# Cross-attention with image tokens on one core: the two parts of Z' summed by the matrix engine, and the image branch's steps moved to later slots

## The chip, the cores and the metric

The kernel runs on one core of one Trainium2 chip. The metric is the device time of one execution in microseconds (us). The engines are named as in the profile: PE is TensorE (PEld its weight loads), DVE is VectorE, ACT is ScalarE, POOL is GpSimd, SP is SyncE, which here issues the DMAs.

## The reference

Two attention layers follow each other. Each takes x (16 samples, 256 positions, 320 channels) and a context (16 samples, 256 rows, 512 channels), has 20 heads of 16 channels, and adds to a text attention a small attention over the context's last rows. The change is in the second layer only, in which 252 rows are text and the last 4 are image rows:

```python
q = heads(hidden_states @ W_q); k_t = heads(text_ehs @ W_k); v_t = heads(text_ehs @ W_v)
probs_t = softmax(q . k_t * scale)                     # per head, 256 x 252
text_out = probs_t @ v_t
k_ip, v_ip = heads(ip_ehs @ W_k_ip), heads(ip_ehs @ W_v_ip)
qsem = l2norm(probs_t @ text_ehs)                      # per head, 256 x 512, row by row
sem = qsem @ l2norm(ip_ehs).T
fused = q . k_ip * scale + 0.5 * sem
out = (text_out + (softmax(fused) * spatial_mask) @ v_ip) @ W_out + b_out + residual
```

The norm of `probs_t @ text_ehs` is needed for every head and position. The kernel does not form that product. It forms the Gram matrix G of the text rows once for each sample, and takes the squared norm as the sum over text rows of P times (G P), where P are the exponentials of the transposed scores.

## The kernel before, in words

`layer1` (line 655 on) runs one queue of instructions for each engine. All of them are written by the same loop over slots t, from T0 to T1, where slot t stands for head s = t of the running count of 16 x 20 = 320 (sample, head) pairs. An engine's order is the order in which its loop body writes things, slot after slot; engines are tied only by semaphore waits. Nothing is planned at run time. `AT` (line 659) gives the slot of each step that is done once for a sample; `due(t, off)` gives the sample that is due. The numbers of `AT` are read modulo 20 below: "slot 12" is the slot of a sample's 20 in which a step falls in the steady state.

In slot t, PE does in this order:

- NAT, the scores of head t+11 (line 736), from which DVE takes the row maxima MX (line 1063)
- every fourth slot (t = 2, 6, 10, 14, 18 modulo 20) the transposition of four heads' maxima into `rows` (line 747). `rows` is the right half of the PSUM bank PV. ACT (line 925) and DVE (line 1082, NH) read it; line 1082 counts semaphore `nm` up
- TR, the transposed scores of head t (line 757); ACT takes the exponential P (line 933) and a rounded copy PH (line 937)
- GP = G P of head t-2, six matmuls through the helper `product` (lines 768 to 772; in the trace they have the helper's line 60). It waits until DVE has read GP of the head before: there is one GP bank
- the group product PV for four heads (lines 773 to 791): 8 matmuls of VB with P into four column groups (line 787), then 4 matmuls of E21 with ZS (line 790), which put the squared norm into column 21 of each head's output. It stands in slots t = 3, 7, 11, 15, 19 modulo 20
- then the steps done once for a sample, on two PSUM banks MISC, taken in turn by a `Ring`: k (line 792), on (line 801), ptt, ipm, hst, om, q, gr, v, scm (lines 809 to 888), in this order within a slot. `take` makes a step wait until the bank's use before last has been read

DVE does in slot t: MX of head t+11, ZP = GP x PM of head t-2 (line 1071), PM = 2P - PH of head t-1 (line 1077), NH where it is due, and then the steps of `AT`. POOL adds the two halves of ZP (the two chunks of 128 text rows) into ZS (line 1221) and does the square roots (`pow`, line 1242), which DVE's `sem` steps (lines 1092 to 1125) wait for, and other subtractions and additions.

The group product's waits are, in order: the exponentials of its four heads, the read of PV by ACT (`pvs`), the count `nm`, and ZS:

```python
e.wait_ge(q["nm"], min(g + 4, B * NGRP))
e.wait_ge(q["zs"], HG * g + HG)
```

The group due at t = 4g + 7 waits for count g + 4 of `nm`. NH of group g + 3 is due at t = 4(g + 3) - 6 = 4g + 6.

Of the kernel before, what the change touches and what calls it, by code (L numbers as in the profile page):

```python
# [8 lines left out]
ALU = mybir.AluOpType  # L9
# [3 lines left out]
B, S, C, CD, H, D = 16, 256, 320, 512, 20, 16  # L13
T = 256
HG = 4
NGRP = H // HG
SLOT = 32
# [4 lines left out]
KC = CD // 128  # L22
# [17 lines left out]
def due_group(t, off):  # L40
    g, r = divmod(t - off, HG)
    return g if r == 0 and 0 <= g < B * NGRP else None
# [33 lines left out]
def stage(flat, n0, k):  # L76
    return flat[:, n0:n0 + k * C].rearrange("p (k n) -> p k n", n=C)
# [577 lines left out]
def layer1(nc, ctx, a, parts_h, vall, x1, x1_t, out):  # L655
    NT, NI, NV = T - 4, 4, D + 6
    N2 = NT - 128
    TRK = KM + 2
    AT = dict(q=(-3, 1, 5), k=(-2, 2, 6), spill=(-1, 3, 7), x_in=-22, xts=-12, c_in=-18, cts=-6, gr=(4, 8), v=(10, 12), kbd=12, scm=14,
              vip_in=20, vip=26, cmb=46, root=(46, 47, 48, 49), sem=(50, 51, 52), fu=53, tx=(54, 55, 56), ptt=56, ipm=59, hst=62, om=(69, 73), out=75,  # L660
              xb_in=59, xb=63)
    ONCE = -12
    NS, NZ, NIP = 4, 6, B * NI

    def sb(name, shape, dt=F32):
        return ctx.enter_context(nc.sbuf_tensor(name + "_1", shape, dt))
# [4 lines left out]
    def bank(name):  # L671
# [9 lines left out]
    MX, NH = sb("MX", [128, 2, 2, 8]), sb("NH", [4, 2, 2, S], F32R)  # L681
    P, PVS = sb("P", [128, NP, 2 * S]), sb("PVS", [128, S])
    PH, PM = sb("PH", [128, NS, 2 * S], F32R), sb("PM", [128, 2, 2 * S])
    ZP, ZS = sb("ZP", [128, 2, 2 * S]), sb("ZS", [128, NZ, S])
    GH, GL = sb("GH", [128, 2, 3, 128], F32R), sb("GL", [128, 2, 3, 128], F32R)
    E21, ONES, HALF = sb("E21", [128, SLOT]), sb("ONES", [128, 128]), sb("HALF", [128, NIP])
    ON = sb("ON", [128, 2, 2, H * NV])
# [10 lines left out]
    PV, GP = bank("PV"), bank("GP")  # L698
    ring = Ring([bank(f"MISC{k}") for k in range(2)])

    q = semaphores(nc, ctx, "s1_", "w_q w_k w_v w_rest w_sel sel x_in c_in xn_in spilled0 spilled1 spilled2 stack0 stack1 stack2 stack3 "
                   "stack4 mrow0 mrow1 store fill clear clear_q w_hi w_lo xt_hi xt_lo ct_hi ct_lo qk qk_f qk_hi qk_lo gr vc gh gl w_ip once once_s once_q rn "
                   "vall_out vip_in kbd scm sc vip vm v nat mx mxt nh nm tr exp ph pm gp zp zs pv pvs ont on cmb nrm fu fexp tx "
                   "ptt pt ipm hs hst ht_hi ht_lo om y xb")
    flat = P[:, :, :].rearrange("p r n -> p (r n)")
    q_raw, k_raw, v_raw = stage(flat, 0, 3), stage(flat, 3 * C, KC), stage(flat, (3 + KC) * C, KC)
    o_raw = stage(PM[:, :, :].rearrange("p r n -> p (r n)"), 0, 3)
    ki_raw = stage(ON[:, :, :, :].rearrange("p b a n -> p (b a n)"), 0, KC)
    vi_raw = stage(ZS[:, :, :].rearrange("p r n -> p (r n)"), 0, KC)
    once = XB[:, :, :].rearrange("p a n -> p (a n)")  # L710
    CIP, SQ = (once[:, n * KC * NIP:(n + 1) * KC * NIP].rearrange("p (k n) -> p k n", n=NIP) for n in range(2))
    VALL = HS[0:NIP, 0, :]
# [9 lines left out]
    def _(e):  # L722
        for t in range(T0, T1):
            s = t + LEAD
            if 0 <= s < B * H:
                b, h = divmod(s, H)
# [8 lines left out]
                for i in range(2):  # L735
                    ins = e.matmul(NAT[s % 2][:, i * T:(i + 1) * T], QS[0:KQ, h, i * 128:(i + 1) * 128],  # L736
                                   KS[0:KQ, h, :], start=True, stop=True)
                ins.then_inc(q["nat"], 1)
            g = due_group(t, HG - LEAD + 1)
            if g is not None:  # L740
# [5 lines left out]
                for i in range(2):  # L746
                    ins = e.transpose(rows[:, i * 128:(i + 1) * 128], MX[:, g % 2, i, 0:4], IDENT[:, :])  # L747
                ins.then_inc(q["mxt"], 1)
            s = t
            if 0 <= s < B * H:  # L750
                b, h = divmod(s, H)
# [4 lines left out]
                for i in range(2):  # L756
                    ins = e.matmul(TR[s % 2][:, i * S:(i + 1) * S], KS[0:TRK, h, i * 128:(i + 1) * 128],  # L757
                                   QS[0:TRK, h, :], start=True, stop=True)
                ins.then_inc(q["tr"], 1)
            s = t - 2  # L760
            if 0 <= s < B * H:
                b, h = divmod(s, H)
                p, k = b % 2, s % NS
# [3 lines left out]
                if s:  # L767
# [2 lines left out]
                product(e, GP[:, 0:S], [(GH[:, p, 0, :], p0), (GL[:, p, 0, :], p0)])  # L770
                product(e, GP[:, S:2 * S], [(GH[:, p, 1, :], p0), (GL[:, p, 1, :], p0), (GH[0:N2, p, 2, :], p1),
                                            (GL[0:N2, p, 2, :], p1)]).then_inc(q["gp"], 1)
            g = due_group(t, HG + 3)
            if g is not None:
                b, hg = divmod(g, NGRP)
                heads = [(j, HG * hg + j, (HG * g + j) % NP) for j in range(HG)]
                if hg == 0:
                    e.wait_ge(q["v"], 2 * (b + 1))
                    e.wait_ge(q["vc"], 2 * (b + 1))
                e.wait_ge(q["exp"], HG * g + HG)  # L780
                if g:
                    e.wait_ge(q["pvs"], g)
                e.wait_ge(q["nm"], min(g + 4, B * NGRP))
                e.wait_ge(q["zs"], HG * g + HG)
                for i in range(2):
                    for j, h, r in heads:
                        e.matmul(PV[SLOT * j:SLOT * (j + 1), 0:S], VB[:, b % 2, i, h, :], P[:, r, i * S:(i + 1) * S],  # L787
                                 start=i == 0, stop=False)
                for j, h, r in heads:
                    ins = e.matmul(PV[SLOT * j:SLOT * (j + 1), 0:S], E21[:, :], ZS[:, (HG * g + j) % NZ, :], start=False, stop=True)  # L790
                ins.then_inc(q["pv"], 1)
            for m, off in enumerate(AT["k"]):
                b = due(t, off)
# [7 lines left out]
            g = due_group(t, HG + 5)  # L801
            if g is not None:
# [3 lines left out]
                for i in range(2):  # L806
                    ins = e.transpose(k[:, i * 128:(i + 1) * 128], PVS[:, i * 128:(i + 1) * 128], IDENT[:, :])  # L807
                ins.then_inc(q["ont"], 1)
            b = due(t, AT["ptt"])
            if b is not None:  # L810
# [3 lines left out]
                for i in range(2):  # L814
                    ins = e.transpose(k[0:80, i * 128:(i + 1) * 128], FU[:, 1, i, :], IDENT[:, :])
                ins.then_inc(q["ptt"], 1)
            b = due(t, AT["ipm"])
# [8 lines left out]
            b = due(t, AT["hst"])  # L826
            if b is not None:
                for i in range(2):
# [4 lines left out]
                    for c, c0 in enumerate(CC):  # L833
                        ins = e.transpose(k[0:CK, c * 128:(c + 1) * 128], HS[:, i, c0:c0 + CK], IDENT[:, :])
                    ins.then_inc(q["hst"], 1)
            for i, off in enumerate(AT["om"]):
                b = due(t, off)
# [8 lines left out]
            for m, off in enumerate(AT["q"]):  # L846
                b = due(t, off)
# [58 lines left out]
    def _(e):  # L906
# [12 lines left out]
        for t in range(T0, T1):  # L919
# [7 lines left out]
            if 0 <= s < B * H:  # L927
# [7 lines left out]
                    e.wait_ge(q["gp"], s - NS + 1)  # L935
                e.wait_ge(q["exp"], s + 1)
                e.copy(PH[:, s % NS, :], P[:, s % NP, :]).then_inc(q["ph"], 1)  # L937
            g = due_group(t, HG + 3)
            if g is not None:
                if g:  # L940
                    e.wait_ge(q["ont"], g)
# [88 lines left out]
    def _(e):  # L1030
# [24 lines left out]
        for t in range(T0, T1):  # L1055
# [8 lines left out]
                                ALU.max).then_inc(q["mx"], 1)  # L1064
            s = t - 2
            if 0 <= s < B * H:
                if s >= 2:
                    e.wait_ge(q["zs"], s - 1)
                e.wait_ge(q["pm"], s + 1)
                e.wait_ge(q["gp"], s + 1)  # L1070
                e.tensor_tensor(ZP[:, s % 2, :], GP[:, :], PM[:, s % 2, :], ALU.mult).then_inc(q["zp"], 1)  # L1071
            s = t - 1
            if 0 <= s < B * H:
                if s >= 2:
# [131 lines left out]
    def _(e):  # L1206
# [4 lines left out]
            e.wait_ge(q["xt_hi"], c + 1)  # L1211
            e.tensor_tensor(XTS[1][0:CK, c, :], XT[0:CK, c, :], XTS[0][0:CK, c, :].bitcast(F32), ALU.subtract).then_inc(q["xt_lo"], 1)
        for t in range(T0, T1):
            s = t - 2
            if 0 <= s < B * H:
                if s == 0:
                    e.wait_ge(q["once"], 2)
                if s >= NZ:
                    e.wait_ge(q["pv"], (s - NZ) // HG + 1)
                e.wait_ge(q["zp"], s + 1)  # L1220
                e.tensor_tensor(ZS[:, s % NZ, :], ZP[:, s % 2, 0:S], ZP[:, s % 2, S:2 * S], ALU.add).then_inc(q["zs"], 1)  # L1221
            for m, off in enumerate(AT["k"]):
                b = due(t, off)
                if b is not None:
# [44 lines left out]
    def _(e):  # L1269
# [44 lines left out]
        for t in range(T0, T1):  # L1314
# [26 lines left out]
            if b is not None:  # L1341
                if b == 0:
                    e.wait_ge(q["vall_out"], 16)
                    e.wait_ge(q["sel"], 16)
                if b >= 2:
                    e.wait_ge(q["ipm"], 2 * (b - 1))
                e.dma_start(VIP[:, b % 2, :], vall[NI * b:NI * b + NI, :].unsqueeze(0).broadcast_to([H, NI, C])).then_inc(q["vip_in"], 16)
# [71 lines left out]
```

## Time and profile before

| | us |
|---|---|
| device time, 3 runs: median (lowest to highest) | 1891.41 (1887.83 to 1893.2) |
| device time of the profiled execution | 1883.8 |
| its span, first to last instruction | 1881.4 |
| PE busy | 1678.2 (89% of the span) |
| DVE busy | 1442.5 (77%) |
| ACT busy | 1038.3 (55%) |
| POOL busy | 869.7 (46%) |
| mean granted TensorE clock | 0.946 of 2.4 GHz |

The span is from the first to the last instruction of one profiled execution; what lies around it is 2.4 us. An engine's busy time is the time in which it had at least one instruction under way. The granted clock is 1 at 2.4 GHz and 0.5 at 1.2 GHz. A label such as GP or MISC is the tile that is written; what follows `<-` is what was read.

### The profile page before, as it was taken

Reading aid. Unit: us, or ns where it says so; the run is one execution under the profiler, and the core shown is the slowest. Engines: PE = TensorE matmul, PEld = TensorE weight load, DVE = VectorE, ACT = ScalarE, POOL = GpSimd, SP = SyncE. Lnnn points to the kernel's source line nnn. Section 1 sums busy time; section 2 is a strip of 40 time slices with the busy share of each in tenths; the row PEclk is TensorE's granted clock in tenths of the full one; section 3 lists DMA queues with packets and bytes.
Section 4 is the critical chain, followed back from the end, with each engine's and each line's share of the span. In section 5 each row is a group of like instructions: output and inputs, shape, how many; then the busy total and the mean of one; then the engine's idle time right before and its main releaser. Section 6 shows DMA issues by size and latency. Waiting matters only on the chain.

```text
span 1881.4 us, 42185 instructions
## 1 busy us (share of the span) xinstructions
PE 1678.2 (89%) x14344; PEld 1479.0 (79%) x14344; DVE 1442.5 (77%) x3732; ACT 1038.3 (55%) x2188; POOL 869.7 (46%) x714
## 2 busy tenths in 40 slices
PE   5999999999999997479899888988988898898985
PEld 4888888888888885468788787877878787887864
DVE  4677777777777776458878887887888788787884
ACT  3566666666666665236556555555555554554551
POOL 4232332333332222455666566556555645655553
PEclk9999999999999999689999999999998998998997
DMA  6334444444444332633223313322331322231210
GB/s 170 106 113 115 123 120 117 120 120 118 118 122 113 116 102 66 177 89 90 57 68 97 86 45 90 90 67 67 87 85 46 91 81 58 74 98 53 60 33 21
DMA packets 186492, 172.65 MB, mean 92 GB/s; under 512 B 25884, under 2 KB 186282, under 8 KB 186282
## 3 DMA queue, kind: packets, MB, share of 16 engines
q1 hardware_dynamic: 186282, 169.97, 32.5%
q8 instruction: 117, 1.92, 0.5%
q14 instruction: 93, 0.76, 0.1%
HBM read 110.19 MB, written 57.59 MB: 89 GB/s over the span
## 4 chain that ended last, share of the span: by engine, by line
PE 31%; DVE 11%; POOL 7%; issue 7%; ACT 3%; SPq 1%; DMA 0%; DVEq 0%; ACTq 0%; POOLq 0%
PE MISC L60 12%; PE GP L60 9%; POOL NRM L1242 3%; PE NAT L736 3%; DVE ZP L1071 3%; DVE PM L1077 2%; PE TR L757 2%; POOL ZS L1221 2%; PE PV L787 2%; DVE MX L1063 1%; PE PV L790 1%; PE MISC L807 1%; PE PV L747 1%; ACT P L933 1%; DVE HS L1150 1%
## 5 line engine op out<-in xcount | busy, mean ns | idle before, releaser
L1221 POOL TENSOR_TENSOR ZS<-ZP 128x256 f32<-128x256 f32 x320 | 312.0, 975 | 402.0 <-DVE ZP L1071 402.0
L314 ACT ACTIVATE P<-TA 128x512 f32<-128x512 f32 x320 | 201.9, 632 | 252.5 <-DVE TA L460 251.9
L60 PE MATMUL GP<-PH,GH 128*128 128x256 f32 (+1 forms) x960 | 262.2, 300 | 86.1 <-DVE ZP L1071 67.9
L1071 DVE TENSOR_TENSOR ZP<-GP,PM 128x512 f32<-128x512 f32 x320 | 219.7, 686 | 68.6 <-PE GP L60 55.1
L60 PEld LDWEIGHTS GP<-PH,GH 128*128 128x128 f32 (+1 forms) x960 | 190.9, 199 | 99.3 <-issue 60.6
L60 PE MATMUL GP<-PH,GL 128*128 128x256 f32 (+1 forms) x960 | 254.6, 292 | 0.0
L1077 DVE SCALAR_TENSOR_TENSOR PM<-P,PH 128x512 f32<-128x512 f32 x320 | 247.0, 772 | 0.0
L1063 DVE TENSOR_REDUCE MX<-NAT 128x2 f32<-128x504 f32 x320 | 215.8, 675 | 19.3 <-PE NAT L736 16.1
L445 DVE TENSOR_REDUCE MX<-NAT 128x2 f32<-128x154 f32 x320 | 101.9, 318 | 167.7 <-PE NAT L142 165.8
L933 ACT ACTIVATE P<-TR 128x512 f32<-128x512 f32 x320 | 190.0, 594 | 58.1 <-PE TR L757 54.2
L460 DVE TENSOR_TENSOR TA<-TR,ST 128x512 f32<-128x512 f32 x320 | 219.2, 686 | 3.0 <-PE TR L162 2.8
L937 ACT CAST PH<-P 128x512 fp32r<-128x512 f32 x320 | 198.4, 620 | 28.2 <-PE GP L60 0.4
L60 PEld LDWEIGHTS GP<-PH,GL 128*128 128x128 f32 (+1 forms) x960 | 193.3, 201 | 0.1
L449 DVE CUSTOM_DVE_ANT_0 TMP<-NAT,SN 128x179 f32<-128x179 f32 x640 | 192.0, 337 | 0.4 <-issue 0.2
L526 POOL TENSOR_TENSOR PARTS<-QKF,PARTS 112x512 fp32r<-112x512 f32 (+1 forms) x48 | 61.4, 1280 | 225.5 <-ACT PARTS L332 225.5
L736 PE MATMUL NAT<-KS,QS 65*128 65x256 f32 x640 | 148.4, 316 | 11.4 <-DVE MX L1063 11.4
L142 PE MATMUL NAT<-KS,QS 65*128 65x256 f32 x640 | 151.3, 319 | 5.4 <-DMA KS<-qk_parts 5.4
L757 PE MATMUL TR<-QS,KS 67*128 67x256 f32 x640 | 139.8, 301 | 0.0
L736 PEld LDWEIGHTS NAT<-KS,QS 65*128 65x128 f32 x640 | 106.1, 200 | 39.8 <-issue 26.1
L162 PE MATMUL TR<-QS,KS 69*128 69x256 f32 x640 | 135.4, 294 | 0.2
L142 PEld LDWEIGHTS NAT<-KS,QS 65*128 65x128 f32 x640 | 103.1, 191 | 39.4 <-issue 21.4
L1242 POOL TENSOR_TENSOR NRM<-NRM,HALF 128x10 f32<-128x10 f32 x64 | 132.0, 2064 | 2.5 <-DVE NRM L1090 2.5
(229 smaller groups left out, 4402.7 us busy)
## 6 DMA issues: line engine op xcount, KB each, us to landing
QS<-qk_parts SPq DMA_DIRECT2D x480, 64.0 KB, 2.7
qk_parts<-PARTS SPq DMA_DIRECT2D x96, 224.0 KB, 2.6
CT<-in_ctx_t SPq DMA_DIRECT2D x32, 512.0 KB, 4.2
KS<-qk_parts SPq DMA_DIRECT2D x240, 64.0 KB, 2.7
KS<-qk_parts SPq DMA_DIRECT2D x240, 63.0 KB, 2.9
qk_parts<-PARTS SPq DMA_DIRECT2D x48, 192.0 KB, 2.3
QS<-NH SPq DMA_DIRECT2D x480, 4.0 KB
qk_parts<-PARTS SPq DMA_DIRECT2D x32, 220.5 KB, 3.9
```

Of the source, the lines that this page charges most:

```text
L60: ins = e.matmul(out, lhs, rhs, start=(n == 0), stop=(n == len(pairs) - 1))
L142: ins = e.matmul(NAT[s % 2][:, i * T:(i + 1) * T], QS[0:KQ, h, i * 128:(i + 1) * 128], KS[0:KQ, h, :], start=True, stop=True)
L314: e.activation(P[:, s % NP, :], TA[:, s % 2, :], ACT.Exp, scale=SCALE).then_inc(q["exp"], 1)
L449: ins = e.tensor_tensor_reduce(TMP[:, k, i, :], v[:, i, NT:T], SN[:, b % 2, i, :], 1.0, -3.0e38, ALU.add, ALU.max, MX[:, g % 2, i, HG + j: ...
L460: e.tensor_tensor(TA[:, s % 2, :], TR[s % 2][:, :], ST[:, b % 2, :], ALU.add).then_inc(q["sum"], 1)
L736: ins = e.matmul(NAT[s % 2][:, i * T:(i + 1) * T], QS[0:KQ, h, i * 128:(i + 1) * 128], KS[0:KQ, h, :], start=True, stop=True)
L933: e.activation(P[:, s % NP, :], TR[s % 2][:, :], ACT.Exp, scale=SCALE).then_inc(q["exp"], 1)
L937: e.copy(PH[:, s % NS, :], P[:, s % NP, :]).then_inc(q["ph"], 1)
L1063: e.tensor_reduce(MX[:, g % 2, :, j], NAT[k][:, :].rearrange("p (a t) -> p a t", a=2)[:, :, 0:NT], AX.X, ALU.max).then_inc(q["mx"], 1)
L1071: e.tensor_tensor(ZP[:, s % 2, :], GP[:, :], PM[:, s % 2, :], ALU.mult).then_inc(q["zp"], 1)
L1077: e.scalar_tensor_tensor(PM[:, s % 2, :], P[:, s % NP, :], 2.0, PH[:, s % NS, :].bitcast(F32), ALU.mult, ALU.subtract).then_inc(q["pm"], 1)
L1221: e.tensor_tensor(ZS[:, s % NZ, :], ZP[:, s % 2, 0:S], ZP[:, s % 2, S:2 * S], ALU.add).then_inc(q["zs"], 1)
```

## The change

- The six ZS buffers and POOL's addition (line 1221) go. DVE's ZP has five buffers instead of two; DVE waits for `pv` instead of `zs` before it writes one again. PE's E21 product runs over both halves of ZP: 8 matmuls for a group instead of 4.
- The group product on PE and ACT's copy of its result are due at `HG + 2` instead of `HG + 3`: t = 4g + 6, one slot earlier. It waits for `zp` instead of `zs`. The wait for `nm` stays as it is.
- Of the steps of `AT`, sem goes from (50, 51, 52) to (52, 53, 54), fu 53 to 55, tx (54, 55, 56) to (56, 57, 58), ptt 56 to 59, ipm 59 to 61, hst 62 to 64, vip 26 to 32. root, cmb, om, out and the others stay.
- SP waits for `vip` of the sample before ahead of the load of VIP.

```diff
--- before.py
+++ after.py
@@ -657,10 +657,10 @@
     N2 = NT - 128
     TRK = KM + 2
     AT = dict(q=(-3, 1, 5), k=(-2, 2, 6), spill=(-1, 3, 7), x_in=-22, xts=-12, c_in=-18, cts=-6, gr=(4, 8), v=(10, 12), kbd=12, scm=14,
-              vip_in=20, vip=26, cmb=46, root=(46, 47, 48, 49), sem=(50, 51, 52), fu=53, tx=(54, 55, 56), ptt=56, ipm=59, hst=62, om=(69, 73), out=75,
+              vip_in=20, vip=32, cmb=46, root=(46, 47, 48, 49), sem=(52, 53, 54), fu=55, tx=(56, 57, 58), ptt=59, ipm=61, hst=64, om=(69, 73), out=75,
               xb_in=59, xb=63)
     ONCE = -12
-    NS, NZ, NIP = 4, 6, B * NI
+    NS, NZ, NIP = 4, 5, B * NI
 
     def sb(name, shape, dt=F32):
         return ctx.enter_context(nc.sbuf_tensor(name + "_1", shape, dt))
@@ -681,7 +681,7 @@
     MX, NH = sb("MX", [128, 2, 2, 8]), sb("NH", [4, 2, 2, S], F32R)
     P, PVS = sb("P", [128, NP, 2 * S]), sb("PVS", [128, S])
     PH, PM = sb("PH", [128, NS, 2 * S], F32R), sb("PM", [128, 2, 2 * S])
-    ZP, ZS = sb("ZP", [128, 2, 2 * S]), sb("ZS", [128, NZ, S])
+    ZP = sb("ZP", [128, NZ, 2 * S])
     GH, GL = sb("GH", [128, 2, 3, 128], F32R), sb("GL", [128, 2, 3, 128], F32R)
     E21, ONES, HALF = sb("E21", [128, SLOT]), sb("ONES", [128, 128]), sb("HALF", [128, NIP])
     ON = sb("ON", [128, 2, 2, H * NV])
@@ -700,13 +700,13 @@
 
     q = semaphores(nc, ctx, "s1_", "w_q w_k w_v w_rest w_sel sel x_in c_in xn_in spilled0 spilled1 spilled2 stack0 stack1 stack2 stack3 "
                    "stack4 mrow0 mrow1 store fill clear clear_q w_hi w_lo xt_hi xt_lo ct_hi ct_lo qk qk_f qk_hi qk_lo gr vc gh gl w_ip once once_s once_q rn "
-                   "vall_out vip_in kbd scm sc vip vm v nat mx mxt nh nm tr exp ph pm gp zp zs pv pvs ont on cmb nrm fu fexp tx "
+                   "vall_out vip_in kbd scm sc vip vm v nat mx mxt nh nm tr exp ph pm gp zp pv pvs ont on cmb nrm fu fexp tx "
                    "ptt pt ipm hs hst ht_hi ht_lo om y xb")
     flat = P[:, :, :].rearrange("p r n -> p (r n)")
     q_raw, k_raw, v_raw = stage(flat, 0, 3), stage(flat, 3 * C, KC), stage(flat, (3 + KC) * C, KC)
     o_raw = stage(PM[:, :, :].rearrange("p r n -> p (r n)"), 0, 3)
     ki_raw = stage(ON[:, :, :, :].rearrange("p b a n -> p (b a n)"), 0, KC)
-    vi_raw = stage(ZS[:, :, :].rearrange("p r n -> p (r n)"), 0, KC)
+    vi_raw = stage(ZP[:, :, :].rearrange("p r n -> p (r n)"), 0, KC)
     once = XB[:, :, :].rearrange("p a n -> p (a n)")
     CIP, SQ = (once[:, n * KC * NIP:(n + 1) * KC * NIP].rearrange("p (k n) -> p k n", n=NIP) for n in range(2))
     VALL = HS[0:NIP, 0, :]
@@ -770,7 +770,7 @@
                 product(e, GP[:, 0:S], [(GH[:, p, 0, :], p0), (GL[:, p, 0, :], p0)])
                 product(e, GP[:, S:2 * S], [(GH[:, p, 1, :], p0), (GL[:, p, 1, :], p0), (GH[0:N2, p, 2, :], p1),
                                             (GL[0:N2, p, 2, :], p1)]).then_inc(q["gp"], 1)
-            g = due_group(t, HG + 3)
+            g = due_group(t, HG + 2)
             if g is not None:
                 b, hg = divmod(g, NGRP)
                 heads = [(j, HG * hg + j, (HG * g + j) % NP) for j in range(HG)]
@@ -781,13 +781,15 @@
                 if g:
                     e.wait_ge(q["pvs"], g)
                 e.wait_ge(q["nm"], min(g + 4, B * NGRP))
-                e.wait_ge(q["zs"], HG * g + HG)
+                e.wait_ge(q["zp"], HG * g + HG)
                 for i in range(2):
                     for j, h, r in heads:
                         e.matmul(PV[SLOT * j:SLOT * (j + 1), 0:S], VB[:, b % 2, i, h, :], P[:, r, i * S:(i + 1) * S],
                                  start=i == 0, stop=False)
-                for j, h, r in heads:
-                    ins = e.matmul(PV[SLOT * j:SLOT * (j + 1), 0:S], E21[:, :], ZS[:, (HG * g + j) % NZ, :], start=False, stop=True)
+                for i in range(2):
+                    for j, h, r in heads:
+                        ins = e.matmul(PV[SLOT * j:SLOT * (j + 1), 0:S], E21[:, :], ZP[:, (HG * g + j) % NZ, i * S:(i + 1) * S],
+                                       start=False, stop=i == 1)
                 ins.then_inc(q["pv"], 1)
             for m, off in enumerate(AT["k"]):
                 b = due(t, off)
@@ -935,7 +937,7 @@
                     e.wait_ge(q["gp"], s - NS + 1)
                 e.wait_ge(q["exp"], s + 1)
                 e.copy(PH[:, s % NS, :], P[:, s % NP, :]).then_inc(q["ph"], 1)
-            g = due_group(t, HG + 3)
+            g = due_group(t, HG + 2)
             if g is not None:
                 if g:
                     e.wait_ge(q["ont"], g)
@@ -1064,11 +1066,13 @@
                                 ALU.max).then_inc(q["mx"], 1)
             s = t - 2
             if 0 <= s < B * H:
-                if s >= 2:
-                    e.wait_ge(q["zs"], s - 1)
+                if s >= NZ:
+                    e.wait_ge(q["pv"], (s - NZ) // HG + 1)
                 e.wait_ge(q["pm"], s + 1)
                 e.wait_ge(q["gp"], s + 1)
-                e.tensor_tensor(ZP[:, s % 2, :], GP[:, :], PM[:, s % 2, :], ALU.mult).then_inc(q["zp"], 1)
+                if s == 0:
+                    e.wait_ge(q["once"], 2)
+                e.tensor_tensor(ZP[:, s % NZ, :], GP[:, :], PM[:, s % 2, :], ALU.mult).then_inc(q["zp"], 1)
             s = t - 1
             if 0 <= s < B * H:
                 if s >= 2:
@@ -1211,14 +1215,6 @@
             e.wait_ge(q["xt_hi"], c + 1)
             e.tensor_tensor(XTS[1][0:CK, c, :], XT[0:CK, c, :], XTS[0][0:CK, c, :].bitcast(F32), ALU.subtract).then_inc(q["xt_lo"], 1)
         for t in range(T0, T1):
-            s = t - 2
-            if 0 <= s < B * H:
-                if s == 0:
-                    e.wait_ge(q["once"], 2)
-                if s >= NZ:
-                    e.wait_ge(q["pv"], (s - NZ) // HG + 1)
-                e.wait_ge(q["zp"], s + 1)
-                e.tensor_tensor(ZS[:, s % NZ, :], ZP[:, s % 2, 0:S], ZP[:, s % 2, S:2 * S], ALU.add).then_inc(q["zs"], 1)
             for m, off in enumerate(AT["k"]):
                 b = due(t, off)
                 if b is not None:
@@ -1342,6 +1338,8 @@
                 if b == 0:
                     e.wait_ge(q["vall_out"], 16)
                     e.wait_ge(q["sel"], 16)
+                if b:
+                    e.wait_ge(q["vip"], b)
                 if b >= 2:
                     e.wait_ge(q["ipm"], 2 * (b - 1))
                 e.dma_start(VIP[:, b % 2, :], vall[NI * b:NI * b + NI, :].unsqueeze(0).broadcast_to([H, NI, C])).then_inc(q["vip_in"], 16)
```

## Rows read from the trace of the kernel before

**Rows 1.** Waits of 900 to 1700 us: us in total, times, longest

```profile
PE MISC L834 <- ACT PARTS L955: 10.6, 12, 0.9
...
PE PV L787 <- POOL ZS L1221: 7.6, 13, 1.3
```

**Rows 2.** Instructions in time (start us, us): PE, slot 7 of two samples

```profile
1217.72 0.41 PE L736 MATMUL NAT<-KS,QS 65*128 65x256 f32 x2
...
1283.32 0.41 PE L736 MATMUL NAT<-KS,QS 65*128 65x256 f32 x2
```

**Rows 3.** In time, PE: the starts of slots 3 and 4

```profile
1272.36 0.48 PE L736 MATMUL NAT<-KS,QS 65*128 65x256 f32 x2
...
1275.15 0.51 PE L736 MATMUL NAT<-KS,QS 65*128 65x256 f32 x2
```

**Rows 4.** Chain of waits (start us, us, what), slot 3

```profile
1273.08 0.71 PE GP L60 x6
1273.79 1.00 PE PV L787 x16
1274.79 0.43 PE PV L790 x8
```

**Rows 5.** In time, PE and DVE: slot 6, from GP's end on

```profile
1281.93 0.28 PE L60 MATMUL MISC<-CTSH,WKH 128*96 128x252 f32 x1
...
1282.23 0.69 DVE L1071 TENSOR_TENSOR ZP<-GP,PM 128x512 f32<-128x512 f32 x1 [0.52 <-PE GP L60]
1282.84 0.68 DVE L1077 SCALAR_TENSOR_TENSOR PM<-P,PH 128x512 f32<-128x512 f32 x1
1283.43 0.41 DVE L1082 SCALAR_TENSOR_TENSOR NH<-PV,NH 4x256 fp32r<-4x256 f32 x1
```

**Rows 6.** In time, PE and DVE: ipm in slot 19; ZP, then the next GP

```profile
1262.26 1.34 PE L825 MATMUL MISC<-VIP,PT 80*128 80x320 f32 x4
...
1264.95 0.69 DVE L1071 TENSOR_TENSOR ZP<-GP,PM 128x512 f32<-128x512 f32 x1
...
1265.78 0.36 PE L60 MATMUL GP<-PH,GH 128*128 128x256 f32 x1 [0.49 <-DVE ZP L1071]
```

**Rows 7.** Groups of instructions of 900 to 1700 us: busy us, mean ns, idle before

```profile
L1157 DVE TENSOR_TENSOR HTL<-MISC,HTH 112x384 fp32r<-112x384 f32 x24 | 13.4, 558 | 16.7 <-ACT HTH L982 15.6
```

**Rows 8.** In time, DVE and PE: slot 12

```profile
1232.65 0.72 DVE L1096 TENSOR_TENSOR NRM<-NRM,RZ 128x40 f32<-128x40 f32 x1 [3.55 <-POOL NRM L1242]
...
1236.08 0.44 PE L60 MATMUL GP<-PH,GH 128*128 128x256 f32 x1 [3.06 <-DVE ZP L1071]
```

**Rows 9.** In time, POOL, DVE, PE: slots 14 to 17

```profile
1246.46 2.38 POOL L1255 TENSOR_TENSOR CTSL<-CT,CTSH 128x1024 fp32r<-128x1024 f32 x1
...
1246.92 2.09 DVE L1134 TENSOR_SCALAR FM<-FM,MASK 128x20 f32<-128x20 f32 x2
...
1250.57 0.36 PE L60 MATMUL GP<-PH,GH 128*128 128x256 f32 x1 [1.46 <-ACT PH L937]
...
1253.14 0.44 PE L60 MATMUL GP<-PH,GH 128*128 128x256 f32 x1 [0.33 <-DVE ZP L1071]
```

**Rows 10.** Chain of waits, behind the last head: line 1134 again

```profile
1865.67 0.39 DVE FM L1134 x2
```

**Rows 11.** Stretches: length, busy PE, PEld, DVE, ACT, POOL, PEclk, DMA share, GB/s

```profile
1232.77:1236.19 3.42, 0.36 (x4) 0.18 (x3) 3.32 (x7) 1.27 (x3) 2.02 (x4) 1.00 0.20 57
1236.19:1239.60 3.41, 3.41 (x15) 3.41 (x16) 3.31 (x7) 0.00 (x0) 1.46 (x2) 0.50 0.00 0
...
1249.84:1253.25 3.41, 1.92 (x13) 1.60 (x14) 3.41 (x6) 1.40 (x3) 1.16 (x2) 1.00 0.41 116
1253.25:1256.67 3.42, 3.42 (x17) 3.42 (x18) 3.40 (x5) 1.12 (x3) 1.40 (x2) 0.50 0.00 0
1270.32:1273.73 3.41, 2.52 (x23) 2.15 (x21) 2.02 (x5) 2.52 (x5) 2.31 (x2) 1.00 0.10 9
1273.73:1277.15 3.42, 3.42 (x41) 2.67 (x41) 2.85 (x5) 2.06 (x4) 2.11 (x2) 1.00 0.78 263
```

## The prediction

> **What bounds the kernel now.** I read three views: the table of waits, the instructions in order of time over one sample's 20 slots (two starts of slot 7 are 65.6 us apart [rows 2]), and stretches with the clock. The reader is to see that PE is nearly always at work and that its losses in a sample stand in a few places. In slot 12 DVE waits for POOL's square roots, and PE then waits 3.06 us for ZP [rows 8]. In slots 14 to 17 DVE is crowded: line 1134's two small instructions take 2.09 us while POOL's CTSL runs, and PE waits 1.46 and 0.33 us [rows 9]; alone the same two take 0.39 [rows 10]. Both places are followed by 3.4 us at granted clock 0.50 [rows 11]. Small losses: the product waits for ZS 7.6 us and hst for a bank 10.6 us in 800 us [rows 1], which is 12.2 samples, so 0.6 and 0.9 us a sample. So the order of PE's queue sets the time, and any new wait in it counts in full.
>
> **The step that decides: the count `nm`.** The group product moves to t = 4g + 6 but still waits for count g + 4 of `nm`. That count is given by NH of group g + 3, which DVE does at t = 4(g + 3) - 6 = 4g + 6. Before, a slot lay between the two; now they stand in the same one. The wait is not a spare: `rows` and the product share the bank PV. In that slot DVE does NH behind ZP and PM, and ZP needs this slot's GP. Slot 6 shows the chain: GP's last matmul has been issued and the next starts at 1281.93; ZP starts at 1282.23, PM at 1282.84, NH at 1283.43 and takes 0.41 [rows 5], so it ends at 1283.84. From a DVE end to PE's start behind it 0.14 pass (ZP ends at 1265.64, GP starts at 1265.78 [rows 6]). The product can start at 1283.98: PE stands still for 2.05 us. Behind it in PE's queue are the rest of the slot (k, v, scm) and the next slot's NAT, TR and GP, so nothing of PE's fills the gap; ACT's copy of PV, and ACT's later steps with it, wait too, but ACT is idle for 45% of the span. Five products a sample: 5 x 2.05 = 10.2 us. The bounds are 0, if something I don't see covers it, and 2.7 where GP itself runs at half clock and so ends 0.7 later (its 0.71 [rows 4] doubled).
>
> **The other costs, for one sample.**
> - E21 over both halves: today's four products take 0.43 us on PE [rows 4]; the same again in each group, 5 x 0.43 = 2.15.
> - Slots 3, 7, 11, 15, 19 lose the product. Slot 3 was 2.79 us long [rows 3], and without 1.43 of it [rows 4] 1.36 would be left. But there is one GP bank: GP 0.71 [rows 4], 0.30 to ZP [rows 5], ZP 0.69 and 0.14 to the next GP [rows 6] make 1.84 us a head at the least. So 0.48 in each of the five can't be had: 2.4. (Below nothing it can't be; 0 if DVE's work there is still delayed from before.)
> - hst comes into slot 4, ahead of gr, and there are two MISC banks: gr's take waits for hst's first bank, which DVE reads in HTL, in this same slot behind ZP and PM. From GP's end: 0.30 + 0.61 + 0.60 [rows 5], HTL 0.56 [rows 7], 0.14: 2.2 us, of which the transpositions cover some 0.8. Taken 1.4, bounds 0 and 2.2.
> - ipm comes into slot 1, between on and q. q's take waits for DVE's read of the first ipm bank, again behind ZP and PM: 1.5, an addition taken like HTL's 0.56, and 0.14, so 2.2 us, covered by on and the ipm products, which take 1.34 with their tail [rows 6]. Taken 1.1 with the wait of the second ipm for on's bank; bounds 0 and 2.2.
> - The later vip, fu and ptt are off PE's path. SP's new wait is for a multiplication that stands 8 slots ahead of the load, and nothing behind it in SP's queue is short of time: 0, at most the 0.8 us that one DMA's issue takes, which no one waits for.
>
> Sum of costs: 10.2 + 2.15 + 2.4 + 1.4 + 1.1 = 17.3.
>
> **The gains, for one sample.** The roots of slots 6 to 9 have until slot 12 instead of 10, and POOL has no ZS between them: the wait of 3.06 goes, and with it a stretch of 3.41 at half clock [rows 8, 11], worth half, 1.7: 4.8. What is late next there is v, which PE does at once. In slots 14 to 17: line 1134 moves to slot 16, away from CTSL, and no ZS runs beside DVE; 1.46 + 0.33 + 1.7 (half of the slow 3.42 [rows 11]) go, and I leave 0.8 for slot 16, where DVE's reduction, reciprocal and 1134 still come on top of the three large ones: 2.7. The waits for ZS and for hst's bank go: 0.6 + 0.9. POOL's 312 us in themselves give nothing. Sum 9.0.
>
> What a page says of POOL beside DVE: the Trainium skill, SBUF — State Buffer, "Who interferes with whom", has it that a DVE instruction with two SBUF inputs and a POOL instruction that reads SBUF shut each other out for the whole instruction. The trace agrees: 2.09 beside CTSL against 0.39 alone. By that rule sem's additions, now in slot 14 with CTSL, can be held up by its 2.4 us; that would fall under PE's product and scm, and the sum would be the same.
>
> **The clock.** The stretch with 3.06 us of waiting and the one between 1249.84 and 1253.25, in which PE had the wait of 0.33 and most of that of 1.46 and was busy for 1.92 us of 3.41 were each followed by half clock; the one with 0.9 of waiting (PE busy 2.52) was not [rows 11]. A wait of 2.05 is nearer to the first two. There are seven new places of over 1 us in a sample. I take four falls, and 1.5 us each (half of 3.41 is 1.7, less what PE would have waited anyway): 6.0. Bounds: none, and seven at 1.7, 11.9.
>
> **The sum.** A sample costs 17.3 - 9.0 = 8.3 us more at full clock, and 6.0 for the clock. The last four products need no further NH, so 76 of 80 groups wait, 15.2 samples: 15.2 x 14.3 = 217. On the profiled execution's own 1883.8 that is 2101. Behind the last head no load stands beside the chain, and one or two ZS of 1 us go: 2100. The median of the runs shown is 7.6 above the profiled one and the three differ by 5.4; I leave that in the range.
>
> **Rivals.**
> - *The clock holds.* Same waits, no falls: 1883.8 + 15.2 x 8.3 = 2010. For it: single waits of 0.9 left the clock whole, and the new ones are apart, with busy slots between them. Against: the waits of 1.46 and 0.33 were enough in slots 16 and 17. The Trainium skill, TensorE: Matmul & The Clock Gate, "HAM oscillation — how this bites in real kernels", warns of idle gaps longer than any of the new waits; by that rule the clock would hold, and it would be this rival. The trace of slots 16 and 17 speaks against the rule. Chance 0.2.
> - *The wait on `nm` is covered,* so the time falls. One mechanism: NH would have to be done by GP's end in its slot. Then 10.2 and the 6.0 go, and a sample changes by 7.1 - 9.0 = -1.9: 1883.8 - 29 = 1855. It decides itself in slots 2, 6, 10, 14, 18: below 0.4 us of wait in each (15.2 x 5 x 0.4 = 30) the kernel is faster. For it: POOL's wait of ZP is gone and DVE is freer. Against: NH stands behind ZP in DVE's order, and ZP can't start before GP ends. Chance 0.05.
> - *The clock stays low for longer:* each new wait falls into a slow stretch and keeps it going, seven falls or more: 1883.8 + 15.2 x (8.3 + 11.9) = 2191. For it: at half clock GP ends later and NH with it. Against: after a slow stretch of full work the clock came back at once. Chance 0.05.
> - *The edit does less than it says:* DVE's crowding in slots 14 to 17 stays (CTSL now beside sem), and a part of the five waits takes the place of waits on ZP that PE had anyway. Then the balance is near nothing to +60: 1885 to 1945. Chance 0.05, a third of it within 0.3% of before.
>
> **How the numbers follow.** The forecast has 0.65, with its own range of 2040 to 2150. The range of 8 in 10 is 2000 to 2155: it takes in the rival of the full clock and leaves out the covered wait, the weak edit and the far end. 0.3% is about what a measurement of this kernel can tell from no change. Faster 0.05, within it 0.02, slower 0.93.
>
> **What would show it.** In the trace of after: the first of line 787's products with 1.9 to 2.1 us of idle time before it, released by DVE NH L1082, about 76 times; the second half of the E21 products adding 0.43; DVE no longer waiting for NRM; L1134 at about 0.4 for two; PE waiting before gr in slot 4 for HTL and before q in slot 1 for HS; a mean clock well under 0.946. A sample's length in the steady state is to be 78 to 81 us. The prediction is wrong if the products start right behind GP, or if the clock stays at 1.00 around them.

## The result and the profile after

The changed kernel takes 2153.49 us (median of 4 runs, 2151.58 to 2171.32) against 1889.62 us before (4 runs, 1886.59 to 1893.2): a ratio of 1.1414, 95% interval 1.1381 to 1.1447. It is slower by 264 us where 209 were forecast (2100 against 1891.41). The median lies at the very end of the range of 2000 to 2155, and the ratio times the 1891.41 on which the forecast stood is 2159, just outside. The profiled execution took 2154.05 us against 1883.8.

From the page of the changed kernel, engines and busy tenths:

```profile
span 2151.9 us, 42844 instructions
PE 1792.0 (83%) x14984; PEld 1538.6 (71%) x14984; DVE 1393.4 (65%) x3732; ACT 1030.2 (48%) x2188; POOL 562.4 (26%) x394
PE   5999999999999847877787787877787877877875
PEclk9999999999999977999889988999888997998887
```

The first layer (the first 14 slices or so) is as it was. In the second, POOL has lost its 312 us of additions, PE works 114 us more and still is busy for a smaller share: 83% instead of 89%.

The groups of instructions over the whole execution (busy us, mean ns, idle time before and its releaser):

```profile
L787 PE MATMUL PV<-P,VB 128*32 128x256 f32 x1280 | 112.6, 479 | 157.5 <-DVE NH L1086 157.5
L791 PE MATMUL PV<-ZP,E 128*32 128x256 f32 x1280 | 120.0, 498 | 0.0
L60 PE MATMUL MISC<-CTSH 128*128 128x256 f32 (+1 forms) x128 | 43.8, 342 | 40.0 <-DVE HTL L1161 40.0
L1081 DVE SCALAR_TENSOR_TENSOR PM<-P,PH 128x512 f32<-128x512 f32 x320 | 264.2, 826 | 0.0
```

The first row is the predicted wait: 157.5 us of PE standing still ahead of the group product, released by NH. Slot 6 in order of time, PE and DVE:

```profile
1411.11 0.28 PE L60 MATMUL GP<-PH,GL 124*128 124x256 f32 x1
...
1411.53 0.69 DVE L1075 TENSOR_TENSOR ZP<-GP,PM 128x512 f32<-128x512 f32 x1 [0.59 <-PE GP L60]
1412.14 0.68 DVE L1081 SCALAR_TENSOR_TENSOR PM<-P,PH 128x512 f32<-128x512 f32 x1
1412.74 0.41 DVE L1086 SCALAR_TENSOR_TENSOR NH<-PV,NH 4x256 fp32r<-4x256 f32 x1
...
1413.39 1.07 PE L787 MATMUL PV<-P,VB 128*32 128x256 f32 x16 [2.00 <-DVE NH L1086]
1414.25 1.07 PE L791 MATMUL PV<-ZP,E 128*32 128x256 f32 x16
```

It is the chain of [rows 5], now with the product at its end. A product begins 0.65 us after NH has begun. The next view is of slots 2 to 4 of the changed kernel, POOL, DVE and PE, where the forecast was too low:

```profile
1479.54 1.27 POOL L1223 TENSOR_TENSOR PARTS<-QKF,PARTS 112x508 fp32r<-112x508 f32 x1 [15.80 <-ACT PARTS L957]
1480.77 1.55 POOL L1227 TENSOR_TENSOR XB<-XB,BIAS 128x640 f32<-128x640 f32 x1
...
1480.23 2.64 DVE L1081 SCALAR_TENSOR_TENSOR PM<-P,PH 128x512 f32<-128x512 f32 x1
...
1484.58 1.01 DVE L1161 TENSOR_TENSOR HTL<-MISC,HTH 112x384 fp32r<-112x384 f32 x2
...
1485.18 0.58 PE L60 MATMUL MISC<-CTSH 128*128 128x256 f32 x1 [3.11 <-DVE HTL L1161]
```

PM, 0.68 us elsewhere [rows 5], takes 2.64: it begins while POOL's PARTS runs and ends 0.55 us behind XB. HTL stands behind it and one more MX, ZP and PM in DVE's queue, and PE waits 3.11 us for it ahead of gr. Last the clock, stretches of the changed kernel (columns as in [rows 11]), with the product at 1442.49 in the first's end:

```profile
1439.40:1442.84 3.44, 1.44 (x18) 1.20 (x20) 3.39 (x8) 1.47 (x3) 0.00 (x0) 0.99 0.00 0
1442.84:1446.25 3.41, 3.41 (x35) 1.83 (x26) 0.33 (x1) 0.20 (x1) 0.00 (x0) 0.51 0.27 99
```

One wait for NH alone is followed by a stretch at half clock, in which the product takes 1.75 us instead of 1.07. Work at half clock loses half of its time, so (1 - mean clock) x span is about what the clock costs: 0.084 x 2151.9 = 181 us after, 0.054 x 1881.4 = 102 before, 79 more. PE's busy time agrees: it grew by 114 us, of which 35 are the second half of the E21 product, whose rows follow in the section on the prediction. The next three stretches are of slots 3 to 6 of one sample; the wait of 3.11 us ahead of gr ends at 1403.62, in the second:

```profile
1398.47:1401.88 3.41, 1.61 (x12) 1.39 (x12) 3.41 (x4) 2.56 (x5) 2.29 (x2) 0.98 0.46 129
1401.88:1405.29 3.41, 1.67 (x8) 1.67 (x9) 2.15 (x5) 0.00 (x0) 0.00 (x0) 0.50 0.44 124
1405.29:1408.71 3.42, 3.42 (x19) 3.42 (x18) 1.08 (x3) 1.75 (x5) 0.00 (x0) 0.52 0.00 0
```

Here one fall lasts for two stretches. Between 900 and 2098 us, 14.3 samples, 78 of 351 such stretches are at half clock, in 58 falls; in the kernel before, between 902 and 1837 us, 14.0 samples, it is 35 of 274, in 25 falls.

### The profile page after: what moved, and what is told of

The parts are those of the page before. It is cut to its first block, busy times and chain, and to the rows that moved or that the text cites. A ratio compares the mean times of both kernels' runs of the same rounds, so it can differ in the third digit from the quotient of the medians.

```text
span 2151.9 us, 42844 instructions
## 1 busy us (share of the span) xinstructions
PE 1792.0 (83%) x14984; PEld 1538.6 (71%) x14984; DVE 1393.4 (65%) x3732; ACT 1030.2 (48%) x2188; POOL 562.4 (26%) x394
## 4 chain that ended last, share of the span: by engine, by line
PE 39%; DVE 14%; ACT 5%; issue 5%; POOL 1%; SPq 1%; DMA 0%; DVEq 0%; ACTq 0%; POOLq 0%
PE MISC L60 14%; PE GP L60 8%; DVE PM L1081 6%; PE PV L787 5%; PE PV L791 5%; DVE ZP L1075 4%; PE NAT L736 3%; ACT PH L939 2%; PE TR L757 2%; ACT P L935 2%; DVE MX L1065 1%; PE MISC L888 1%; DVE NH L1086 1%; ACT NH L927 1%; PE PV L747 1%
## 5 line engine op out<-in xcount | busy, mean ns | idle before, releaser
L60 PE MATMUL GP<-PH,GH 128*128 128x256 f32 (+1 forms) x960 | 267.9, 306 | 62.9 <-DVE ZP L1075 61.4
L1081 DVE SCALAR_TENSOR_TENSOR PM<-P,PH 128x512 f32<-128x512 f32 x320 | 264.2, 826 | 0.0
L787 PE MATMUL PV<-P,VB 128*32 128x256 f32 x1280 | 112.6, 479 | 157.5 <-DVE NH L1086 157.5
L1223 POOL TENSOR_TENSOR PARTS<-QKF,PARTS 112x508 fp32r<-112x508 f32 (+1 forms) x48 | 61.0, 1271 | 693.7 <-ACT PARTS L957 693.7
L945 ACT COPY PVS<-PV 128x256 f32<-128x256 f32 x80 | 29.8, 372 | 329.9 <-PE PV L791 329.9
L787 PEld LDWEIGHTS PV<-P,VB 128*32 128x32 f32 x1280 | 46.0, 124 | 187.4 <-issue 180.2
L142 PE MATMUL NAT<-KS,QS 65*128 65x256 f32 x640 | 150.8, 318 | 4.8 <-DMA KS<-qk_parts 4.6
L736 PE MATMUL NAT<-KS,QS 65*128 65x256 f32 x640 | 140.8, 305 | 11.2 <-DVE MX L1065 11.2
L1238 POOL TENSOR_TENSOR NRM<-NRM,HALF 128x10 f32<-128x10 f32 x64 | 137.4, 2164 | 37.6 <-DVE NRM L1094 37.6
```

The source lines that it names most:

```text
L60: ins = e.matmul(out, lhs, rhs, start=(n == 0), stop=(n == len(pairs) - 1))
L1081: e.scalar_tensor_tensor(PM[:, s % 2, :], P[:, s % NP, :], 2.0, PH[:, s % NS, :].bitcast(F32), ALU.mult, ALU.subtract).then_inc(q["pm"], 1)
```

## The experiments

Each is timed against the kernel before on the same chip. From chip to chip the kernel before took 1887 to 1894 us, so a difference between medians of two experiments is good to some 7 us; where it matters, compare the ratios. "NH" is the step at line 1082 of the kernel before.

**e1: NH ahead of ZP and PM in DVE's order, in the changed kernel.**

```diff
@@ block.vector, behind the reduction to MX
+            g = due_group(t, HG - LEAD + 1)
+            if g is not None:
+                e.wait_ge(q["nh"], g + 1)
+                e.scalar_tensor_tensor(NH[0:4, g % 2, 1, :], rows, -1.0, NH[0:4, g % 2, 0, :].bitcast(F32), ALU.mult, ALU.subtract).then_inc(q["nm"], 1)
             s = t - 2
...
@@ block.vector, behind PM
-            g = due_group(t, HG - LEAD + 1)
-            if g is not None:
-                e.wait_ge(q["nh"], g + 1)
-                e.scalar_tensor_tensor(NH[0:4, g % 2, 1, :], rows, -1.0, NH[0:4, g % 2, 0, :].bitcast(F32), ALU.mult, ALU.subtract).then_inc(q["nm"], 1)
```

> The changed kernel with DVE's NH (and so the count nm) put ahead of ZP and PM in its slot; nothing else moves. Theory (the product's wait for nm in its own slot is the loss): the idle time ahead of the product, 157 us in all, falls to under 20 us, some of the clock falls go with it, and the time drops from 2153 to 1900-1990 us. Rival (the doubled E21 product and the bank waits of the moved steps are the loss, and nm only shows it): the time stays above 2110 us.

Measured: 1971.34 us (1962.42 to 1976.82), ratio 1.0427 (1.0392 to 1.0461). The product's group and slot 6:

```profile
L787 PE MATMUL PV<-P,VB 128*32 128x256 f32 x1280 | 87.2, 389 | 34.5 <-DVE NH L1070 26.3 <-ACT P L935 8.2
```

```profile
1410.74 0.41 DVE L1070 SCALAR_TENSOR_TENSOR NH<-PV,NH 4x256 fp32r<-4x256 f32 x1
...
1411.40 1.07 PE L787 MATMUL PV<-P,VB 128*32 128x256 f32 x16 [0.21 <-ACT P L935]
```

The order of two DVE steps alone is worth 182 us of the 264. PE's idle time there falls from 157.5 to 34.5 us, 123 less. Its busy time falls from 1792.0 to 1737.6 us, 54 less for the same work, since the mean clock is 0.940 instead of 0.916. Together that is the 177 us between the two profiled spans. The time is in the expected range, but more of the wait is left than the 20 us expected.

**e2: the kernel before with only the product and ACT's copy one slot earlier.**

```diff
-            g = due_group(t, HG + 3)
+            g = due_group(t, HG + 2)     # on PE and on ACT
```

> The kernel before with the group product and the copy of its result one slot earlier (t = 4g + 6), and nothing else: POOL's addition, the single E21 product and all slots of AT stay. Theory: each product waits about 2.05 us for nm, the slots it leaves are held to 1.84 us by the one GP bank, and the clock falls more often: 2060-2150 us from 1890. Rival (the single early slot is harmless without the other edits): 1880-1900 us.

Measured: 2171.2 us (2167.02 to 2174.11), ratio 1.15 (1.1471 to 1.1528). It is 21 us above the expected range. This one number of the slot makes all of the loss and more, with POOL's addition, the single E21 product and the old slots in place.

```profile
L787 PE MATMUL PV<-P,VB 128*32 128x256 f32 x1280 | 103.8, 446 | 186.1 <-POOL ZS L1221 182.1 <-DVE NH L1082 4.0
```

```profile
1404.72 1.03 POOL L1221 TENSOR_TENSOR ZS<-ZP 128x256 f32<-128x256 f32 x1 [2.40 <-DVE ZP L1071]
...
1405.09 0.41 DVE L1082 SCALAR_TENSOR_TENSOR NH<-PV,NH 4x256 fp32r<-4x256 f32 x1
...
1405.75 1.07 PE L787 MATMUL PV<-P,VB 128*32 128x256 f32 x16 [2.00 <-POOL ZS L1221]
```

The view names ZS, since that addition ended last (1405.75). But it is the addition for a head of the next group, which this product does not ask for, and the product begins 0.66 us after NH begins, as it does in the changed kernel, which has no ZS. So I read the releaser as NH here too; it is a reading of the times, no run takes ZS out of this kernel. A wait of several semaphores is put down to the last event near it, and this is how it misleads.

**e3: the new slots alone, in the kernel before.**

```diff
-              vip_in=20, vip=26, ... sem=(50, 51, 52), fu=53, tx=(54, 55, 56), ptt=56, ipm=59, hst=62, ...
+              vip_in=20, vip=32, ... sem=(52, 53, 54), fu=55, tx=(56, 57, 58), ptt=59, ipm=61, hst=64, ...
```

> The kernel before with the new slots of AT (sem, fu, tx, ptt, ipm, hst, vip and SP's wait) and nothing else. Theory: the waits for the square roots and in slots 14 to 17 go with their slow stretches (8.4 us a sample), new bank waits before gr and q come (about 3.9 us a sample): 1810-1860 us. Rival (the moves cost more than they bring): 1890-1930 us.

Measured: 1884.19 us (10 runs), ratio 0.9974 (0.9954 to 0.9995): next to nothing, a miss of 24 us and more. The waits of 1000 to 1700 us, and slots 2 to 4 of one sample, POOL first, then DVE and PE:

```profile
PE MISC L60 <- DVE HTL L1157: 30.6, 11, 2.9
PE GP L60 <- DVE ZP L1071: 29.2, 37, 2.0
```

```profile
1018.32 1.29 POOL L1227 TENSOR_TENSOR PARTS<-QKF,PARTS 112x508 fp32r<-112x508 f32 x1 [0.61 <-ACT PARTS L955]
1019.56 0.74 POOL L1221 TENSOR_TENSOR ZS<-ZP 128x256 f32<-128x256 f32 x1
1020.25 1.56 POOL L1231 TENSOR_TENSOR XB<-XB,BIAS 128x640 f32<-128x640 f32 x1
1019.02 3.33 DVE L1077 SCALAR_TENSOR_TENSOR PM<-P,PH 128x512 f32<-128x512 f32 x1
1024.67 0.39 PE L60 MATMUL MISC<-CTSH 128*128 128x256 f32 x1 [2.90 <-DVE HTL L1157]
```

DVE's wait for the roots, 3.55 us in a sample before [rows 8], is gone from the list, but the bank wait ahead of gr costs 2.8 us a sample, and the mean clock is 0.938, no better than 0.946. What the roots gave went into the wait that the moves made. PM of slot 3 is held up here too, for 3.33 us beside PARTS, ZS and XB, although POOL has its addition ZS as before.

**e4: the changed kernel with the old slots of AT** (the diff of e3 the other way round).

> The changed kernel with all slots of AT as before. Theory: the waits for the roots have been hidden by now, since POOL has no addition and the slots are longer, so the moves bring nothing here and the bank wait before gr (3.1 us a sample) goes: 2090-2140 us. Rival (the moves are still worth what they are worth in the kernel before): 2200 us or more.

Measured: 2093.01 us (2091.27 to 2097.66), ratio 1.1091 (1.1065 to 1.1116). In the changed kernel the moves cost 60 us. Without them the wait ahead of gr is gone: PE is idle for 39 us less (321.0 against 359.9) and busy for 23 us less, at a mean clock of 0.930. DVE does wait for the roots again, 2.2 us in a sample, but no wait of PE for ZP between 1000 and 1700 us is longer than 1.3 us, where the kernel before has 3.1.

**e5 and e11: POOL's addition to XB two slots later, and two slots earlier, in the changed kernel.**

```diff
-              xb_in=59, xb=63)
+              xb_in=59, xb=65)      # e5
+              xb_in=59, xb=61)      # e11
```

> The changed kernel with POOL's addition of the bias to XB two slots later (slot 5 instead of 3), nothing else. Theory (PM in slot 4 waits 2 us for POOL's PARTS and XB, which run one behind the other, and HTL and gr wait behind it): PM of slot 4 falls to about 1.1 us at most, the wait ahead of gr from 3.1 to about 1.5 us a sample, the time from 2153 to 2105-2135 us. Rival (HTL is late for its own reasons, ACT's HTH or the banks): the wait stays near 3.1 and the time within 10 us of 2153.

> The changed kernel with POOL's addition to XB ahead of PARTS of slot 2 in POOL's queue (slot 1 instead of 3), nothing else. In e5 it was put behind, and as nothing else stood in POOL's queue it ran right behind PARTS all the same. Theory (PM of slot 3 waits for PARTS and XB one behind the other): that PM falls from 2.64 to about 1.1 us, the wait ahead of gr from 3.1 to about 1.6 us, the time from 2153 to 2110-2140 us. Rival (PM's length is not what holds gr): the wait stays at 3.1 us and the time within 12 us of 2153.

Measured: e5 2165.39 us (2165.18 to 2168.0), ratio 1.1438 (1.141 to 1.1466); e11 2137.86 us (2136.23 to 2147.22), ratio 1.1324 (1.1291 to 1.1356). gr's group and PM, of e5 and then of e11:

```profile
L60 PE MATMUL MISC<-CTSH 128*128 128x256 f32 (+1 forms) x128 | 43.8, 342 | 40.0 <-DVE HTL L1161 40.0
L1081 DVE SCALAR_TENSOR_TENSOR PM<-P,PH 128x512 f32<-128x512 f32 x320 | 261.9, 818 | 0.0
```

```profile
L60 PE MATMUL MISC<-CTSH 128*128 128x256 f32 (+1 forms) x128 | 39.6, 309 | 20.3 <-DVE HTL L1161 20.3
L1081 DVE SCALAR_TENSOR_TENSOR PM<-P,PH 128x512 f32<-128x512 f32 x320 | 241.3, 754 | 0.0
```

e5 changed nothing (its interval of the ratio overlaps that of the changed kernel), because it changed no order: between slots 2 and 5 nothing else stands in POOL's queue and the data of XB is long there, so XB ran right behind PARTS as before. e11 changes the order, and the wait ahead of gr falls from 40.0 to 20.3 us, the time by 16, both as expected. So PM's hold-up beside PARTS and XB together is half of that wait. (It is the PM of slot 3, not of slot 4 as the text for e5 has it.)

**e6: the changed kernel with the product back at t = 4g + 7.**

```diff
-            g = due_group(t, HG + 2)
+            g = due_group(t, HG + 3)     # on PE and on ACT
```

> The changed kernel with the group product and ACT's copy back at t = 4g + 7; five ZP buffers, E21 over both halves and the moved steps stay. ZP of head 4g + 5 then waits for the product in its own slot. Theory (the slot is the loss, not the doubled product): no wait for nm, a wait of a few tenths of a us for ZP in its place: 1890-1950 us. Rival (with five buffers the ZP wait takes nm's place in full): over 2050 us.

Measured: 1857.68 us (1854.89 to 1867.62), ratio 0.9822 (0.9788 to 0.9856): faster than the kernel before by 1.8%, and 32 us under the range of its theory, which said where the loss is but not how much the other edits bring once it is gone. The waits of 1000 to 1700 us:

```profile
DVE ZP L1075 <- PE PV L791: 83.1, 44, 2.2
PE GP L60 <- DVE ZP L1075: 30.1, 67, 1.0
PE MISC L60 <- DVE HTL L1161: 14.3, 11, 1.3
PE MISC L60 <- DVE HS L1154: 5.0, 11, 0.5
```

With five buffers ZP does wait for the product, up to 2.2 us; but PE is at work on that product meanwhile, and the row that counts is PE's own, the second: 30.1 us in 700 of waiting for ZP. The mean clock is 0.965, and none of the 269 stretches of 3.41 us between 901 and 1819 us is at half clock. So the slot, and not what was put into it, was the loss: 296 us.

**e7: the kernel before with e3's slots, but ipm=60 and hst=63.**

```diff
-              ... ptt=59, ipm=61, hst=64, ...
+              ... ptt=59, ipm=60, hst=63, ...
```

> The kernel before with the new slots of AT, but ipm at 60 and hst at 63 instead of 61 and 64, so that neither shares a slot with gr or q. Theory (the moves alone gave nothing because the bank waits before gr and q, 3.2 us a sample, ate what the roots gave back): those two waits are gone and the time is 1815-1855 us from 1884. Rival (the moves give nothing by themselves): 1875-1890 us.

Measured: 1823.37 us (1815.23 to 1825.11), ratio 0.9623 (0.9594 to 0.9652). The wait for HTL falls to 13.0 us in 700, that for HS is gone, the clock is 0.956.

**e8: e1 with ipm=60 and hst=63.**

> The kernel of e1 (NH ahead of ZP and PM) with ipm at 60 and hst at 63. Theory: the bank waits go here too, 3.5 us a sample with what they do to the clock: 1890-1930 us from 1971. Rival (they are covered here by the longer slots): 1955-1975 us.

Measured: 1910.46 us (1904.88 to 1911.37), ratio 1.0085 (1.006 to 1.0111). 61 us less than e1, as in e7 against e3. It is still slower than before by 0.9%. PE's idle time is no longer the reason (198.8 us, 203.2 before); its busy time is 33 us longer (1710.7 against 1678.2), about what the second half of the E21 product takes. With the product in this slot PE still waits 19.3 us in 700 for HTL ahead of gr and 16.9 for NH; the next kernel has neither wait.

**e9: e6 with ipm=60 and hst=63.**

> The kernel of e6 (product back at t = 4g + 7, five ZP buffers, E21 over both halves) with ipm at 60 and hst at 63. Theory (the doubled product costs little where the order is right, and the bank waits of 1.9 us a sample are the last loss of the moves): 1805-1835 us from 1858. Rival (the doubled product, 34 us, keeps it behind e7): 1840-1860 us.

Measured: 1810.33 us (1807.94 to 1813.57), ratio 0.9584 (0.9558 to 0.961). Neither bank wait is in PE's list, and the clock is 0.976. It is the fastest kernel here, 4.2% under the kernel before; its interval overlaps that of e7, so whether giving up POOL's addition is worth anything is not settled.

**e10: e6 with the E21 product over the first half of ZP alone.**

```diff
-                for i in range(2):
+                for i in range(1):
                     for j, h, r in heads:
-                        ... start=False, stop=i == 1)
+                        ... start=False, stop=True)
```

> The kernel of e6 with the E21 product over the first half of ZP alone, 4 matmuls a group instead of 8; the second half of the squared norm is left out. Theory (the second half costs its 0.43 us on PE, 80 times, since the slot's chain PV, ZP, GP runs through it): 34 us less, 1815-1830 us from 1858. Rival (it stands beside DVE's work and costs nothing): within 8 us of 1858.

Measured: 1842.76 us (1836.54 to 1847.59), ratio 0.975 (0.9721 to 0.9779), 15 us less than e6. Neither theory: of the second half's 34 us about half shows. PE is busy for 34 us less (1662.7 against 1696.5) but idle for 13 more (182.6 against 169.2). The intervals of e6 and e10 lie only just apart (0.9779 and 0.9788), so 15 is rough.

**e12: e9 with xb=61 and cts=-5.**

> The kernel of e9 with two of POOL's steps moved: the addition to XB to slot 1, ahead of PARTS, and CTS to slot 15, behind DVE's small steps with two SBUF inputs of slot 14 (line 1129 takes 1.97 us beside CTSL there in e9, 0.33 alone). Theory (DVE's time beside POOL's reads is still on the path in slots 14 and 3): PE's waits for ZP, 22 us in 700, fall by a third or more and the time is 1795-1806 us from 1810. Rival (they are covered by the product's slot): within 4 us of 1810.

Measured: 1821.0 us (5 runs, 1816.48 to 1826.76), ratio 0.9646 (0.9623 to 0.9668), 11 us more than e9. A miss: PE's waits for ZP rose to 27.3 us in 700 instead of falling. Which of the two moves does it was not tried.

## Why the mechanism was right and the size short

The mechanism and the place were right, and so was the size of the main term. Five waits of 2.05 us a sample for `nm`, 10.2 x 15.2 = 155 us in all, measured 157.5; e1 and e6 take it away from both sides, and e2 makes it in the kernel before. Of the rivals, the covered wait is out by the first row of the profile after, and with it the edit that does less than it says. That the clock holds is out as well: one wait of 2.00 us was followed by half clock. With it the Trainium skill's rule (TensorE: Matmul & The Clock Gate, "HAM oscillation — how this bites in real kernels"), which warns only of longer gaps, does not hold in this case.

The rival of a clock that stays low for longer is right in part: a third of the falls last for two stretches.

The gap is 53 us: 270 between the profiled executions where the sum gave 217. PE's idle time went from 203.2 to 359.9 us, its busy time from 1678.2 to 1792.0, and the terms share that out (of the gains of 9.0 a sample, 5.6 are waits and 3.4 clock). The E21 product in the kernel before, and over both halves in e9, where two of 251 stretches are at half clock:

```profile
L790 PE MATMUL PV<-ZS,E 128*32 128x256 f32 x640 | 49.8, 380 | 0.0
L791 PE MATMUL PV<-ZP,E 128*32 128x256 f32 x1280 | 84.5, 381 | 0.0
```

| term of the sum | forecast, us in all | measured, us in all |
|---|---|---|
| waits for `nm` | 10.2 x 15.2 = 155 | 157.5 |
| E21 over both halves | 2.15 x 15.2 = 33 | 84.5 - 49.8 = 35 |
| wait ahead of gr | 1.4 x 15.2 = 21 | 40.0 |
| wait in slot 1 | 1.1 x 15.2 = 17 | 6.0 |
| other idle time of PE: GP bank, less the waits that go | (2.4 - 5.6) x 15.2 = -49 | 156.7 - 157.5 - 40.0 - 6.0 = -47 |
| clock, net of what goes | (6.0 - 3.4) x 15.2 = 40 | 113.8 - 34.7 = 79 |

- **The step that failed is the clock**, "I take four falls, and 1.5 us each". Of the 53 us it has 39. The number of falls was right, 58 in 14.3 samples or 4.1 a sample. The price was not: 78 stretches at half clock, each worth half of its 3.41 us, are 9.3 us a sample and 2.3 us a fall, because 20 of the 58 falls are followed by a second stretch at half clock. In 13 of these 20 PE stood still again in the first one, as in the rows above; in the other seven it was busy for 2.95 us and more, and why the clock stayed low there is open. In the kernel before the same count gives 4.3 us a sample, so the net is 5.0 us a sample (5.2 by the table, 79 / 15.2) and not 2.6. The bound of 11.9 for the new falls would have held it, but the range stopped at 2155, short of the 2191 that this bound gives.
- **The wait ahead of gr**, forecast 1.4 with a bound of 2.2, is 3.1 us in the steady state. The chain was counted with PM at its undisturbed time. What I left out is that the PM in this chain runs beside POOL's PARTS and XB. That POOL has lost ZS is not the reason: with ZS in place e3 has the same wait, 2.90 us. The Trainium skill (SBUF — State Buffer, "Who interferes with whom") has the rule that a DVE instruction with two SBUF inputs and a POOL instruction that reads SBUF shut each other out, and I weighed it for the edit's gain, at sem and CTSL, and not for the new chain. The trace agrees in PM, 2.64 us against 0.68. Line 1134, where the prediction sees the rule, is a less clear case: its two inputs are one tensor and one column of MASK. In e11, with XB out of the way, 20.3 us are left: the forecast of 21 holds for an undisturbed chain.
- **The gains** were credited to the moves at 4.8 and 2.7 us a sample. In the kernel before they are real only with ipm and hst elsewhere (e7: 71 us under the kernel before on its chip; e3: nearly nothing). In the changed kernel the stalls of [rows 8, 9] are gone as forecast, so the sum stands; but the moves were not needed for that, since without them PE's longest wait for ZP is 1.3 us and the kernel is 60 us faster (e4).

A sample takes 84 us on average (286 of its 320 MX stand in the 1200 us from 900 on) where the prediction has 78 to 81. By the same count it is 67 us in the kernel before (280 in the 940 us from 900 on), and not the 65.6 of the one sample that the prediction read.

## What to carry to other kernels

A step moved one slot earlier keeps its semaphore counts: for each wait that it takes along, look up the slot of the instruction that gives the count. If it is now the same slot, the whole chain inside the slot becomes idle time of an engine whose queue runs in order. Then look at the other end: putting the giver first in its engine's slot was worth 182 us here, and the slot back 296. And when a moved step brings a new chain, count each link at the time that it takes in that slot, beside what the other engines do there: PM was counted at 0.6 us and took 2.64.

## What the runs showed of the hardware

- A PM of DVE, with two SBUF inputs, that began beside POOL's additions lasted until they were over, two or three of them if they followed at once. It took 2.64 us beside PARTS and XB and 3.33 in e3 beside PARTS, ZS and XB, and no PM took more than 1.31 us in e11, where PARTS and XB are apart. POOL's square roots did not do this: three of them ran from 1419.34 to 1425.73 in the changed kernel, and the PMs at 1421.04 and 1423.24 took 0.68 us each.
- TensorE's mean granted clock fell as PE's waits grew, but not in step with them: 0.946 before with 203 us of idle time, 0.976 in e9 with 137, 0.916 with the waits for NH (360), and 0.894 in e2 (364). In e2 the clock costs about (1 - 0.894) x 2166.9 = 230 us, more than the waits ahead of the product themselves, 186.
- Four E21 matmuls more in each group, 34 us of PE's time in all, showed as 15 us in e10, with PE busy for 91% of e6's span.
